# Full-width transfers of context and keys, and paired small operations in a slot attention, in a four-layer kernel on one core

## What is computed

```
x = x + tanh(g) * xattn0(layernorm(x), ctx, masks)     # 16 heads, q @ k, softmax over ctx rows, @ v
x = x + tanh(g) * ffn0(layernorm(x))
slots = layernorm(x)                                   # (16, 56, 128)
Pn = rmsnorm(ctx, w_in); k = Pn @ Wk.T; v = Pn @ Wv.T
for _ in range(3):
    q = rmsnorm(slots, w_slot) @ Wq.T
    attn = softmax(q @ k.T * D**-0.5, over the 56 slots)
    attn = attn / (sum over the 1500 rows + eps)
    slots = gru(attn @ v, slots)      # r, z = sigmoid(...); n = tanh(xn + r * (h @ Whn.T + bhn))
x = x + tanh(g) * slots
x = x + tanh(g) * ffn1(layernorm(x))
```

## Time and profile before

| | |
|---|---|
| timed runs | 602.22 us median of 3 (599.32 to 603.02) |
| profiled execution | 600.12 us; its span 598.3 us |
| busy in the span | PE 486.3, DVE 383.1, ACT 323.6, POOL 220.9 us |
| mean granted clock of TensorE | 0.93 of full speed |
| context statistics and planning | 0 to 83 us |
| attention items | 83 to 160 us |
| first experts | 174 to 250 us |
| slot attention | 254 to 483 us |
| second experts, output | 484 to 598 us |
| transfers | 74.5 MB, 124 GB/s in the mean |

### The profile page before, as it was taken

How to read it: one execution, slowest core, us unless ns; L and a number is a source line. 1 busy time by engine, 2 the same in 40 slices (tenths; PEclk the granted TensorE clock), 3 DMA queues, 4 the chain that set the end, 5 groups by cost and what they waited for, 6 DMA issues and landing times.

```text
span 598.3 us, 17867 instructions
## 1 busy us (share of the span) xinstructions
PE 486.3 (81%) x6388; PEld 363.2 (61%) x6388; DVE 383.1 (64%) x1149; ACT 323.6 (54%) x959; POOL 220.9 (37%) x414
## 2 busy tenths in 40 slices
PE   4878778788696999879989997889999676959990
PEld 2422225554573454478878887778888645849980
DVE  0789855565627454478989998889899736013332
ACT  2654843444411122398998996889889431023330
POOL 7477741222420000135445554454454300712241
PEclk9998988999897799999999998999999867969996
DMA  8996643343139992600000799100000198130003
GB/s 279 219 227 182 182 145 99 107 118 113 51 123 288 279 210 64 281 3 3 3 3 0 218 315 269 30 4 2 3 0 1 54 424 366 52 87 19 22 29 105
DMA packets 30590, 74.48 MB, mean 124 GB/s; under 512 B 6853, under 2 KB 22198, under 8 KB 29510
## 3 DMA queue, kind: packets, MB, share of 16 engines
q1 hardware_dynamic: 26380, 61.87, 36.1%
q0 software_dynamic: 1424, 7.81, 3.5%
q10 hardware_dynamic: 2730, 4.03, 2.2%
HBM read 69.17 MB, written 4.54 MB: 123 GB/s over the span
## 4 chain that ended last, share of the span: by engine, by line
PE 35%; DVE 34%; issue 8%; POOL 7%; DMA 7%; ACT 5%; POOLq 1%; DVEq 1%; ACTq 1%; SPq 0%
DVE ps L1198 6%; DVE sm L1209 6%; PE ps L1537 4%; PE ps L1738 4%; PE ps L1752 3%; DMA work<-in_kv_blk 3%; PE ps L1571 2%; POOL work L708 2%; PE ps L1592 2%; PE ps L1620 2%; POOL xe_scratch L747 2%; DVE sumsq L992 2%; PE ps L1445 2%; ACT work L860 2%; PE ps L1474 2%
## 5 line engine op out<-in xcount | busy, mean ns | idle before, releaser
L860 ACT ACTIVATE work<-ps,nb,rkey 125x56 f32<-125x56 f32 x576 | 173.6, 473 | 3.2 <-DVE nb L1201 3.2
L1620 PE MATMUL ps<-region,work 125*64 125x129 f32 x1152 | 75.7, 280 | 16.2 <-POOL work L708 16.1
L1606 PE MATMUL ps<-work,region 128*61 128x56 f32 (+1 forms) x2304 | 76.7, 221 | 6.6 <-issue 5.1
L1606 PEld LDWEIGHTS ps<-work,region 128*61 128x61 f32 (+1 forms) x2304 | 74.8, 137 | 11.4 <-issue 7.8
L1620 PEld LDWEIGHTS ps<-region,work 125*64 125x64 f32 x1152 | 64.6, 139 | 22.1 <-POOL work L708 21.4
L708 POOL TENSOR_TENSOR work<-work,rs 125x336 f32<-125x336 f32 x96 | 72.0, 750 | 7.5
L706 POOL TENSOR_TENSOR rs<-rs,rkey 125x6 f32<-125x6 f32 x96 | 19.4, 202 | 100.7 <-DVE rs L1213 100.6
L1198 DVE TENSOR_REDUCE ps<-ps 125x6 f32<-125x336 f32 x96 | 48.5, 505 | 3.0 <-PE ps L1606 2.8
L1209 DVE TENSOR_REDUCE sm<-work 125x6 f32<-125x336 f32 x96 | 47.4, 494 | 2.7 <-ACT work L860 2.7
L1592 PE MATMUL ps<-GI,work 112*64 112x112 f32 (+3 forms) x288 | 35.3, 318 | 7.4 <-DVE work L1222 3.2
L1445 PE MATMUL ps<-xln,folded 128*128 128x448 f32 x64 | 29.2, 580 | 6.9 <-ACT region L787 6.9
(11 more groups left out here) (302 smaller groups left out, 1014.5 us busy)
## 6 DMA issues: line engine op xcount, KB each, us to landing
region<-in_w SPq DMA_DIRECT2D x6, 2048.0 KB, 18.3
region<-in_ctxT SPq DMA_DIRECT2D x16, 750.0 KB, 12.3
region<-in_ctx_wide SPq DMA_DIRECT2D x16, 677.2 KB
early_w<-in_ctx SPq DMA_DIRECT2D x16, 672.0 KB
work<-in_ctxT_blk SPq DMA_DIRECT2D x22, 187.5 KB
early_w<-in_w POOLq DMA_DIRECT2D x1, 4096.0 KB, 12.4
region<-in_ctx_blk ACTq DMA_DIRECT2D x11, 187.5 KB
early_w<-in_ctx_blk ACTq DMA_DIRECT2D x10, 187.5 KB
```

Of the source, the lines that this page charges most:

```text
L860: i = act.activation(shares_of(p, a, h)[:, c, :], ps[:CP, 2 + 2 * a + h, c * S:(c + 1) * S], ACT.Exp, bias=nb[:, a, q:q + 1], scale=rkey[: ...
L1606: mm = pe.matmul(ps[r0:r1, 2 + 2 * a + h, c * S:(c + 1) * S], keysT[:, s, c0 + r0:c0 + r1], qT[:, p, a * S:(a + 1) * S], start=True, stop= ...
L1620: mm = pe.matmul(ps[i * COL:(i + 1) * COL, bank, 0:KW], A[:CP, p % 2, i, h, c * S:c * S + COL], keys[:, 2 * p + i, h * CH + c, :], start=( ...
```

## The change

Four parts.

1. Transfers. The host pads the context, its blocks and the wide keys with three rows, so that each is 128 partitions. One transfer of 128 takes the place of two (112 and 13 partitions) for the context and the wide keys, and of one of 125 for an item's plain rows. Work on them still uses 125 partitions.
2. Pairs. The negation, the reciprocal and the product with the scale are done once for both texts of a half (125x2x6 elements) instead of twice. The PSUM banks of the steps are renumbered so that the two of a half are neighbours.
3. The third gate's bias is added by TensorE (a row of ones times the bias row, into the same PSUM), and VectorE's operation and its buffer go. The candidate reads the sum from PSUM.
4. New sequences of the phases on all engines. Scores run 4 steps ahead (all of the next unit) and both updates stand at the end of TensorE's phase.

```diff
-                for p0, p1 in ((0, 112), (112, CP)):
-                    sp.dma_start(dst[p0:p1, :], ctx_b[bass.ds(b, 1), p0:p1, :].rearrange("a p c -> (a p) c")).then_inc(done, 16)
+                sp.dma_start(dst, t["ctx"][bass.ds(b, 1), :, :].rearrange("a p c -> (a p) c")).then_inc(done, 16)
...
-                        for p0, p1 in ((0, 112), (112, CP)):
-                            sp.dma_start(keys[p0:p1, s, :, :].rearrange("p c d -> p (c d)"),
-                                         t["ctx_wide"][g * GB + s, p0:p1, :]).then_inc(ld_keys[p], 16)
+                        sp.dma_start(keys_all[:, s * CC * KW:(s + 1) * CC * KW], t["ctx_wide"][g * GB + s]).then_inc(ld_keys[p], 16)
...
-                act.dma_start(ictx[k][:KP, :, :], t["ctx_blk"][bass.ds(blk, 1), :, :].rearrange("a (p c) d -> (a p) c d", c=KC)).then_inc(ld_item[k], 16)
+                act.dma_start(ictx[k], t["ctx_blk"][bass.ds(blk, 1), :, :].rearrange("a p (c d) -> (a p) c d", c=KC)).then_inc(ld_item[k], 16)
...
+            def weights(g, p, v_, m):
+                b, c, h = both(g, p, m)
+                n = v_ * STEPS + m
+                gp.wait_ge(a_rec, v_ * TWO_HALVES + (h + 1))
+                gp.tensor_tensor(rs[:, :, c], rs[:, :, c], rkey[:, b, c], ALU.mult).then_inc(a_w, 1)
+                gp.wait_ge(a_w, v_ * TWO_HALVES + (h + 1))
...
+                weights(g, p, v_, 0)
+                weigh(p, v_, 0)
+                weigh(p, v_, 1)
                 if renews(g, c):
                     slot_rms(v_ + 2, c % 2)
-                weigh_ahead(4)
+                weights(g, p, v_, 2)
+                weigh(p, v_, 2)
+                weigh(p, v_, 3)
...
-                v.tensor_scalar(hn, ps[:, 1, QS:2 * QS], bhh[:, 2:3], None, ALU.add).then_inc(hn_ok, 1)
-                v.scalar_tensor_tensor(tmp, rt, 1.0, hn, ALU.add, ALU.mult).then_inc(gru_v, 1)
+                v.scalar_tensor_tensor(tmp, rt, 1.0, ps[:, 1, QS:2 * QS], ALU.add, ALU.mult).then_inc(gru_v, 1)
...
-                by_columns(ps[:, 1, QS:2 * QS], whh[:, 2 * D:3 * D], slots_x[:, p, :]).then_inc(ut_mm, 1)
+                by_columns(ps[:, 1, QS:2 * QS], whh[:, 2 * D:3 * D], slots_x[:, p, :], stop=False, skip_group_check=True)
+                by_columns(ps[:, 1, QS:2 * QS], bhn[:, :], ones[0:1, 0:QS], start=False, skip_group_check=True).then_inc(ut_mm, 1)
...
-                scores_ahead(3)
                 scores_ahead(4)
                 scores_ahead(5)
                 if cell_runs(g, c):
                     gru_start(v_ - 1, (c - 1) % TWO)
-                update(g, c % TWO, v_, 0, 6 + c % 2)
                 if renews(g, c):
                     slot_proj(v_ + 2, (c + 2) % TWO, 6 + (c + 1) % 2)
                 scores_ahead(6)
+                scores_ahead(7)
                 if cell_runs(g, c):
                     gru_gates(v_ - 1)
-                update(g, c % TWO, v_, 1, 6 + c % 2)
+                update(g, c % TWO, v_, 0, 6 + c % 2)
                 if renews(g, c):
                     queries(v_ + 2, 6 + (c + 1) % 2)
+                update(g, c % TWO, v_, 1, 6 + c % 2)
```

More of the change, by code:

```diff
@@ L254, in build_program @@
         qT = qT_all.rearrange("p (a s) -> p a s", a=TWO)
-        Un, rt, zt, nt, hn, tmp = (carve(QS, "work") for _ in range(6))
+        Un, rt, zt, nt, tmp = (carve(QS, "work") for _ in range(5))
         Pn = carve(128, "work")
@@ L464, in step_of, with both @@
             return 2 * p + i, h, i
+        def both(g, p, m):
+            h = m // 2
+            return slice(g * GB + 2 * p, g * GB + 2 * p + 2), slice(h * CH, (h + 1) * CH), h
         def cell_runs(g, c):
@@ L1189, in _, with maxima, negated, sums @@
             v.wait_ge(hb_ok, 2)
-            def maxima(g, p, v_, m):
+            def maxima(p, v_, m):
                 s, h, a = step_of(p, m)
-                b, n = g * GB + s, v_ * STEPS + m
-                c = slice(h * CH, (h + 1) * CH)
-                mx = ps[:CP, 2 + 2 * a + h, 400:400 + CH]
+                n = v_ * STEPS + m
                 v.wait_ge(a_mm, n + 1)
-                v.tensor_reduce(mx, ps[:CP, 2 + 2 * a + h, 0:CH * S].rearrange("p (c s) -> p c s", s=S),
+                v.tensor_reduce(ps[:CP, 2 + 2 * h + a, 400:400 + CH],
+                                ps[:CP, 2 + 2 * h + a, 0:CH * S].rearrange("p (c s) -> p c s", s=S),
                                 AX.X, ALU.max).then_inc(a_max, 1)
-                v.wait_ge(a_max, n + 1)
-                v.scalar_tensor_tensor(nb[:, a, c], mx, -1.0, rkey[:, b, c], ALU.mult, ALU.mult).then_inc(a_neg, 1)
-            def attention(g, p, v_, m):
+            def negated(g, p, v_, m):
+                b, c, h = both(g, p, m)
+                v.wait_ge(a_max, v_ * STEPS + (m + 2))
+                v.scalar_tensor_tensor(nb[:, :, c], ps[:CP, 2 + 2 * h:4 + 2 * h, 400:400 + CH], -1.0, rkey[:, b, c],
+                                       ALU.mult, ALU.mult).then_inc(a_neg, 1)
+            def sums(p, v_, m):
                 s, h, a = step_of(p, m)
@@ L1209, in attention, with reciprocals @@
                 v.tensor_reduce(sm[:, a, c], shares_of(p, a, h), AX.X, ALU.add).then_inc(a_sum, 1)
-                v.wait_ge(a_sum, n + 1)
+            def reciprocals(p, v_, m):
+                b, c, h = both(0, p, m)
+                n = v_ * STEPS + m
+                v.wait_ge(a_sum, n + 2)
                 if not isinstance(n, int) or n >= 4:
-                    v.wait_ge(a_att, n - 3)
-                v.reciprocal(rs[:, a, c], sm[:, a, c]).then_inc(a_rec, 1)
+                    v.wait_ge(a_att, n - 2)
+                v.reciprocal(rs[:, :, c], sm[:, :, c]).then_inc(a_rec, 1)
             def update(v_, bank):
@@ L1269, in _ @@
                 queries(x, x, 6 + (x + 1) % 2)
-            for m in range(LOOK):
-                maxima(0, 0, 0, m)
-            attention(0, 0, 0, 0)
+            for m in (0, 2):
+                maxima(0, 0, m)
+                maxima(0, 0, m + 1)
+                negated(0, 0, 0, m)
+            sums(0, 0, 0)
             def phase(g, c, v_):
                 old = (c - 2) % TWO
+                p = c % TWO
                 def maxima_ahead(m):
@@ L1279, in maxima_ahead, with negated_ahead @@
                     if to:
-                        maxima(to[0], to[1], v_ + to[2], to[3])
+                        maxima(to[1], v_ + to[2], to[3])
+                def negated_ahead(m):
+                    to = steps_ahead(g, c, m)
+                    if to:
+                        negated(to[0], to[1], v_ + to[2], to[3])
                 def sums_ahead(m):
@@ L1284, in sums_ahead @@
                     if to:
-                        attention(to[0], to[1], v_ + to[2], to[3])
+                        sums(to[1], v_ + to[2], to[3])
                 if (g, c) != (0, 0) and (c == 0 or renews(g, c - 1)):
                     queries(v_ + 1, (c + 1) % TWO, 6 + c % 2)
+                sums_ahead(1)
                 if cell_runs(g, c):
                     update(v_ - 1, 6 + (c + 1) % 2)
-                maxima_ahead(3)
-                sums_ahead(1)
-                maxima_ahead(4)
-                sums_ahead(2)
+                reciprocals(p, v_, 0)
                 if cell_ends(g, c):
@@ L1661, in _ @@
                 queries(x, 6 + (x + 1) % 2)
-            for m in range(LOOK):
+            for m in range(STEPS):
                 scores(0, 0, 0, m)
```

69 lines of the change are left out of this document (33 added, 36 removed).

## The result

The changed kernel takes 569.35 us (median of 4, 568.20 to 571.25) against 600.95 for the kernel before (median of 4 beside it). The ratio is 0.9476, with a 95% interval of 0.9431 to 0.9520. That is 31.6 us faster, where 22 were forecast and 571 was the lower end of the range: right in direction, and too small by more than the range allowed. The profiled execution's span fell from 598.3 to 567.2 us.

A forecast was written before the change was run, and what follows sets the result against it. Item loop bound by transfers with no engine full, slot attention by VectorE, first among three nearly full engines. 600.1 - 9.2 (items) - 12.5 (slot attention) = 578.4, plus 2.1 to the median's scale: 580 us; range 571 to 591.

The forecast's parts named there:

- rival A: Slot attention: GpSimd's back-to-back weighings hold up one more VectorE slot operation; unit 8.6 us, total 590; chance 0.17.
- (C): Slot attention: GpSimd ends last in each unit, delaying the second update; unit 9.15 to 9.8 us; chance 0.04.
- (B): Item loop: VectorE's and ScalarE's running-maximum steps take over at 3.3 us or more; gain 3, total 586; chance 0.13.
- The two loops: Item loop: transposed-context loads at 2.97 us an item, context rows at 3.01, both against 3.44 before; saving 9.2 us.
- I put both at 0: Wide keys' and first-stage context transfers: no gain, as hidden; 1 to 2 us if some wait sat behind them.
- sized 8.2: Slot attention: the new unit near 8.2 us instead of 8.81; 12.5 us gained after start and end.
- ScalarE's 8.08: Slot attention: ScalarE's need per unit, 8.81 less its 0.73 us wait for TensorE's gates, unchanged by the change.
- TensorE, put at 8.1 to 8.4: Slot attention: TensorE's need per new unit in us, including 0.26 for the bias's four short matmuls.
- 1.5 us lost were forecast: Slot attention, start and end: first exponential waits for two maxima (+0.5), last unit's weighings come late (+0.8 and +0.2).
- 8.81 - 0.98 = 7.83: Slot attention: VectorE's need per new unit, less 0.74 us from paired operations and 0.24 from the third gate's bias.
- VectorE all 8.81: Slot attention before: VectorE has no idle time and needs the whole steady unit of 8.81 us.
- 15.3 and 12 us: Both stages: their better bounds, taken in part as gains, given for the range's lower end of 571 us.

The follow-up runs named there:

- t_all: The kernel before with all three kinds of transfers at 128 partitions and nothing else of the change: 590.22 us, ratio 0.976 to the kernel before.
- s_only: The changed kernel with the transfers of before (112 and 13 partitions, 125 for an item): 591.71 us, ratio 0.978 to the kernel before.
- no_reload: The kernel before without loading the second group's keys, so its output is not the reference's: 597.76 us, ratio 0.996 to the kernel before.
- t_item: The kernel before with only the items' plain rows at 128 partitions: 595.09 us, ratio 0.982 to the kernel before.

## Why the prediction missed

**Right.** The two stages and what bounded them; the count of packets, 144 a transfer instead of 130, which fits 5 engines for 125 rows; ScalarE as the new bound, with its wait gone and VectorE idle instead; one slot operation held up by GpSimd (0.78 us) and no second one in the steady unit, so rival A did not come there (line 1260, which stands in 8 of the 24 units, does lose 0.37 us in the median); no slower unit (C), and no floor of 3.3 us in the item loop (B).

**The item loop: a term too small by 2.0 us.** The two loops were put at 2.97 and 3.01 us; 2.91 was measured. Part of the difference was not in my sum: a transfer of 125 rows takes ScalarE 507 ns to issue, one of 128 rows 339 (lines 816 of before and 820 of after, minima of their issues on ScalarE):

```profile
L816 ACTq DMA_DIRECT2D region<-in_ctx_blk x11: 507/508/575, 81.0 to 155.5; - x11
```

```profile
L820 ACTq DMA_DIRECT2D region<-in_ctx_blk x11: 339/339/393, 81.7 to 146.1; - x11
```

**The keys' transfers: the step that failed.** "But nothing of the steady unit waits for them: its chain has only engines in it. [...] I put both at 0, and at 1 to 2 us gained if some wait sat behind them." For the steady unit this was right. But the sum took 8.81 us for all units, while the stage has 230.2 / 24 = 9.6 us per unit, and I did not look at those that were longer. Several lay in 329 to 377 us, where the keys came in; of the 5.1 us that TensorE waited for its own instructions, 4.5 stood there, and its clock fell there. The transfers' width gave 5.1 to 5.4 us in the slot attention by the traces of t_all and s_only, and some 3 to 5 by the medians (no_reload; t_all against t_item).

**The unit: sized 8.2, was 7.97.** Two reasons. ScalarE's 8.08 was its period less its idle time; but its row before the gap, the reading of an accumulator, was counted to its end, 0.37 us, and where the next operation is ready it takes 0.22 (284.70 to 284.92 above). And I added 0.1 to ScalarE's figure for three engines that run nearly full. That room was not needed: TensorE, put at 8.1 to 8.4, keeps within 7.97 with the four matmuls more. 23 units x 0.23 are 5.3 us.

**Start, end and irregular units: 1.5 us lost were forecast, 2.5 came.** From the first scores to the first update it was 7.2 us and is 10.2; from the last update to the last slots 9.1 and 6.4; that is 0.3 lost in both. But 23 x 0.84 = 19.3 us would be the gain if all units had shortened as the steady one, and 16.8 is measured beside the transfers. The rest of the loss lies in units that are not steady.

**The wrong credit.** The sum argued the shorter unit from VectorE's operations: 8.81 - 0.98 = 7.83. The runs show that in the new order the operations' share is zero and the sequences give the whole. "VectorE all 8.81", as a need, was the step that failed here: 1.2 us of it stood behind a maximum or a sum whose next reader came at once, and went away when the order put something between. I had priced that only where operations were merged.

In numbers, on the spans: 21.7 us were forecast and 31.1 came. The forecast lacks 5.4 for the keys, 5.3 for the unit and 2.0 for the items; against that, start, end and irregular units lost 1.0 more than I had, and the stages outside both got 2.3 us longer (0.7, 0.3 and 1.3 in the table), which I had at 0. The two steps that took the result out of the range are the keys at 0 and the unit at 8.2. The range itself had a slip: the bounds it names, 15.3 and 12 us, come to 600.1 - 27.3 + 2.1 = 575, not 571.

## What to carry to other kernels

A transfer of 125 partitions is not nearly one of 128 (4.5 against 3.0 us here): pad to 128, and do it also where the transfer is hidden, since here the keys' transfers cost 3 to 6 us in units whose chain doesn't name them. Where engines run near 90% each, first put other work between an operation and the one that needs it: here the order alone gave all of that part, and the merging nothing on top. And size a stage by its whole length over its units, not by a steady one alone.

## What I had not expected of the hardware

The same wide keys move at 280 GB/s as 112 + 13 partitions and at 400 GB/s as 128, with the DMA engines 0.96 and 0.98 busy. A packet takes longer: 210 of them filled 16 engines for 4 us in one case and for 3 us in the other, which is 0.29 against 0.22 us in the mean. Why is not shown.

A stall of 2.70 us on TensorE cost more than its length: the granted clock was 0.50 for some 3.4 us behind it.

Issuing costs by shape too: 507 ns on ScalarE for 125 partitions by 3 runs, 339 for 128 by one. This run changed both the partitions and the runs per partition, so which of the two it is stays open.
